# Layer norm in two parts, query weights behind x in one DMA queue, and edge counts from ScalarE signs, in a graph transformer layer

## Chip, cores, metric

One core of a Trainium2 chip runs the whole program. The metric is device time in microseconds. The kernel before was timed three times: 259.06, 259.42 and 260.69 us, median 259.42.

## What is computed

625 nodes with 256 features each, and 20,000 edges (src, dst), sorted by dst. The reference, cut to what matters:

```python
edge_index = jnp.stack([src, dst])
xn = _layernorm(x, axis=-1)                      # (x - mean) / sqrt(var + 1e-5)
x = x + gnn(xn, edge_index, W_l, W_r, b_r) + mix(xn[None], Wqkv, bqkv, Wproj, bproj, temperature)[0]
x = x + ffn(_layernorm(x, axis=-1)[None], W1, b1, Wg, bg, Wd, bd)[0]

# gnn: mean over incoming edges
sums = segment_sum(x[src], dst); counts = segment_sum(ones, dst)
out = (sums / maximum(counts, 1)) @ W_l.T + x @ W_r.T + b_r
# mix: qkv = x @ Wqkv.T + bqkv, 8 heads of 32; q and k normalised per head;
#   a Taylor-like attention: sums over nodes of (1 + s + s*s/2) * v, over the same without v; then Wproj
# ffn: H = gelu(x @ W1 + b1); gate = softmax(H @ Wg + bg); each row takes its best of 8 experts
```

## The kernel before

The nodes stand in T = 5 tiles of 125 rows. The program is written by hand for each engine: each engine has one list of instructions, and semaphores tie them. SyncE and ScalarE issue the loads.

**Front (0 to about 15 us).** SyncE loads the edges, ScalarE loads x; when x is there, SyncE issues w_qkv (L376), b_qk, w_lr and the rest. VectorE turns src and dst into floats (L653, L654), makes half_src, which ScalarE's steps need (L655), and then the first layer norm for all five tiles at once: BN_STATS (L659), BN_AGGR (L662), variance plus epsilon (L664), ScalarE's square root (L523), reciprocal (L670) and the normalised rows `xn` (L672, tile `row` in the profile). Between them VectorE makes `ge` (L666, a part of `at_sb`): for k = 1 to 4, whether each dst is at least 125 k. TensorE transposes xn (L915, two tiles of nodes at a time), ScalarE copies each part to xnT (L528), and TensorE multiplies by w_qkv (L922).

**Projections.** For t = 0 to 4 the q and k columns (`projected(t, ...)`, two 512-wide float32 products, four matmuls in the profile), then for t = 0 to 4 the v columns with W_l's. They go round four PSUM banks; so the last of the v projections needs the bank that ScalarE's first copy to vz (L535) empties. VectorE adds the bias to q and k (L694, `biased`), ScalarE squares them (L516, `square`), VectorE sums the squares by head (L699, `head_sums`), ScalarE takes the roots of the norms (L538, L539) and VectorE makes them factors and scales q and k (L723 to L733).

**Which tiles a group of edges touches.** Behind the first projection TensorE multiplies a column of ones by `ge` (L937, five matmuls summed), which gives for each of 32 groups of 625 edges how many have dst at or past each tile's start. VectorE reads the sums (L712, L713), GpSimd turns them into codes (L445 to L465), and TensorE branches on these.

**One-hot products (33 to 99.8 us).** The segment sum is a product of one-hot matrices. For each group g of 5 x 125 edges, VectorE writes five one-hot matrices of dst and two step matrices of src (L681, L684), and ScalarE three step matrices by a Sign (L501: +1 or -1 as a column is past src or not), in a ring of seven buffers in `mem`. Both call this `fill(g)`; ScalarE's fill of a group may start when TensorE has used the group seven earlier (semaphore oh_free). TensorE works in 16 pairs of groups (L958, L960, ending in L986). Between the pairs stand jobs of the attention, all through PSUM bank 7: `sums` (L992), which VectorE reads at L741 and L742, then five transposes of q and k (L999, ScalarE's copy L546), four products L1016 (VectorE's L751), and four L1021 (ScalarE's L554). Each job waits till the reader before has emptied the bank. After the last pair (L1024) the sums are complete.

ScalarE's list from the end of the front on is this:

```python
act.wait_ge(half_ready, 1)
step_rows(0, 0, 2)
act.wait_ge(var_ready, 1)
nc.scalar.activation(rstd[:, :], rstd[:, :], ACT.Sqrt).then_inc(std_ready, 1)
step_rows(0, 2, act_steps(0)).then_inc(steps_ready, 1)
...
for t in range(T):
    fill(1 + t)
    square(t)
for t in range(T):
    act.wait_ge(qkv_ps, T + t + 1)
    nc.scalar.copy(vz[:, t, 0:2 * C], ps[0:TP, QKV_BANKS[(T + t) % 4], :]).then_inc(vz_ready, 1)
...
for g in range(T + 1, AHEAD):
    fill(g)
```

The attention, the second layer norm and the experts follow and aren't touched.

## Time and profile before

| | us |
|---|---|
| median of three runs | 259.42 |
| the profiled execution | 260.61 |
| its span, first to last instruction | 258.6 |
| TensorE busy | 238.5 |
| VectorE busy | 146.5 |
| ScalarE busy | 143.1 |
| GpSimd busy | 33.1 |

Spans of instructions overlap where an engine works in a pipeline, so the step from one start to the next is often shorter than the duration of one. TensorE is busy nearly always, but that is an average; what counts is, in each stretch, who was waited for last. The timelines show it: each line has the start, the duration, the instruction, and in brackets how long the engine had stood idle and which instruction it had waited for. A line of the timeline can hold several like instructions (x5). The granted clock is TensorE's, as a share of 2.4 GHz; 0.5 is the lower level of 1.2 GHz.

### The profile page before, as it was taken

Reading aid. Unit: us, or ns where it says so; the run is one execution under the profiler, and the core shown is the slowest. Engines: PE = TensorE matmul, PEld = TensorE weight load, DVE = VectorE, ACT = ScalarE, POOL = GpSimd, SP = SyncE. Lnnn points to the kernel's source line nnn. Section 1 sums busy time; section 2 is a strip of 40 time slices with the busy share of each in tenths; the row PEclk is TensorE's granted clock in tenths of the full one; section 3 lists DMA queues with packets and bytes.
Section 4 is the critical chain, followed back from the end, with each engine's and each line's share of the span. In section 5 each row is a group of like instructions: output and inputs, shape, how many; then the busy total and the mean of one; then the engine's idle time right before and its main releaser. Section 6 shows DMA issues by size and latency. Waiting matters only on the chain.

```text
span 258.6 us, 4709 instructions
## 1 busy us (share of the span) xinstructions
PE 238.5 (92%) x1428; PEld 147.7 (57%) x1429; DVE 146.5 (57%) x418; ACT 143.1 (55%) x213; POOL 33.1 (13%) x63
## 2 busy tenths in 40 slices
PE   7599989989998989999999999998899999999990
PEld 3336647555554544433358885544355568888880
DVE  2968799999999955991114566700810242332220
ACT  3679666999999984899971014424015333332000
POOL 7007400000000005600000000000270000000331
PEclk9889999999999999999999999999999999999998
DMA  4760000000000000069950000030034000000111
GB/s 129 276 216 0 3 1 5 3 3 4 5 3 3 3 5 0 3 237 423 426 218 4 0 0 0 6 128 27 0 92 118 0 1 3 0 1 3 32 31 39
DMA packets 6030, 15.82 MB, mean 61 GB/s; under 512 B 2724, under 2 KB 3783, under 8 KB 4723
## 3 DMA queue, kind: packets, MB, share of 16 engines
q1 hardware_dynamic: 4576, 13.43, 13.9%
q0 software_dynamic: 1280, 1.31, 1.9%
q10 hardware_dynamic: 144, 0.66, 0.6%
q8 instruction: 21, 0.34, 0.6%
q14 instruction: 9, 0.07, 0.1%
HBM read 14.08 MB, written 1.30 MB: 59 GB/s over the span
## 4 chain that ended last, share of the span: by engine, by line
PE 62%; ACT 25%; DVE 8%; DMA 2%; issue 1%; POOL 0%; DVEq 0%
ACT mem L501 21%; PE ps L1223 16%; PE ps L1155 11%; PE ps L1043 7%; PE ps L1064 5%; PE ps L1121 4%; PE ps L1206 3%; PE ps L958 3%; PE ps L1112 2%; PE ps L1114 2%; DMA edges_sb<-in_edges 2%; PE ps L922 1%; PE ps L1131 1%; DVE qk_sb L733 1%; DVE mem L681 1%
## 5 line engine op out<-in xcount | busy, mean ns | idle before, releaser
L501 ACT ACTIVATE mem<-ids_m,half_src 125x628 bf16<-125x628 f16 x96 | 69.8, 817 | 5.1 <-DVE half_src L655 3.0
L958 PE MATMUL ps<-mem 125*128 125x501 bf16 x180 | 50.8, 374 | 4.3 <-issue 2.9
L681 DVE TENSOR_SCALAR mem<-node_ids,dst_f 125x628 bf16<-125x628 f16 x160 | 51.7, 369 | 0.0
L1223 PE MATMUL ps<-mem 128*125 x192 | 41.6, 379 | 0.0
L960 PE MATMUL ps<-mem 125*128 125x126 bf16 x180 | 39.3, 218 | 0.0
L1223 PEld LDWEIGHTS ps<-mem 128*125 128x125 f32 x192 | 36.0, 188 | 5.4
L958 PEld LDWEIGHTS ps<-mem 125*128 x180 | 17.6, 98 | 26.8 <-issue 10.2
L570 ACT ACTIVATE qk_sb<-ps,sc_col 125x626 f32<-125x626 f32 (+1 forms) x40 | 28.6, 779 | 3.7 <-PE ps L1043 3.7
L1155 PE MATMUL ps<-xnT,w_sb 128*128 128x512 f32 (+1 forms) x104 | 28.8, 435 | 0.1
L684 DVE TENSOR_SCALAR mem<-ids_m,src_f 125x628 bf16<-125x628 f16 x64 | 23.6, 369 | 0.0
L1155 PEld LDWEIGHTS ps<-xnT,w_sb 128*128 128x128 f32 x104 | 15.9, 191 | 13.2 <-issue 12.9
L615 ACT ACTIVATE mem<-ps,b_sb 128x625 f32<-128x625 f32 x14 | 11.0, 783 | 20.4 <-PE ps L1155 20.1
L1043 PE MATMUL ps<-mem 32*125 32x313 f32 (+1 forms) x160 | 19.1, 472 | 0.2 <-DVE mem L760 0.2
L636 ACT COPY mem<-mem 128x1000 f32 x8 | 8.2, 1031 | 19.8 <-PE ps L1223 19.8
L960 PEld LDWEIGHTS ps<-mem 125*128 x180 | 17.5, 97 | 1.5
L893 DVE SCALAR_TENSOR_TENSOR row<-vz,row x12 | 5.8, 486 | 20.1 <-issue 20.1
L484 POOL DMA_INDIRECT rows_sorted<-row,pos x5 | 6.2, 1238 | 78.9 <-DVE pos L851 77.7
L922 PE MATMUL ps<-wqkv_sb,xnT 128*125 128x512 f32 (+1 forms) x40 | 15.8, 536 | 0.0
L878 DVE COPY mem<-mem 128x500 f32 (+2 forms) x12 | 4.1, 393 | 20.3 <-ACT mem L615 19.9
L1064 PE MATMUL ps<-qk_sb,vz 125*32 125x313 f32 (+1 forms) x160 | 14.7, 439 | 0.6 <-ACT qk_sb L570 0.6
L1043 PEld LDWEIGHTS ps<-mem 32*125 32x125 f32 x160 | 8.9, 180 | 10.5 <-issue 5.0
L489 POOL DMA_INDIRECT out<-row,node_u x5 | 5.9, 1189 | 55.5 <-DVE row L896 55.5
(200 smaller groups left out, 265.0 us busy)
## 6 DMA issues: line engine op xcount, KB each, us to landing
mem<-in_wd SPq DMA_DIRECT2D x8, 1024.0 KB, 12.9
w_sb<-in_w SPq DMA_DIRECT2D x1, 1024.0 KB, 8.7
vz<-in_bd SPq DMA_DIRECT2D x1, 1000.0 KB
wqkv_sb<-in_w_qkv SPq DMA_DIRECT2D x1, 768.0 KB, 4.2
x_all<-in_x ACTq DMA_DIRECT2D x1, 640.0 KB, 4.5
row<-rows_sorted SPq DMA_DIRECT2D x1, 579.7 KB
wlr_sb<-in_w_lr SPq DMA_DIRECT2D x1, 512.0 KB, 6.0
bqk_all<-in_b_qk SPq DMA_DIRECT2D x1, 256.0 KB, 5.2
```

The costliest lines, as they stand in the source:

```text
L501: ins = nc.scalar.activation(oh[:, g % OHB, 0, j, :], ids_m1[:, :], ACT.Sign, bias=half_src[:, g * GC + j:g * GC + j + 1])
L570: nc.scalar.activation(gsq[:, u % NGB, :, 0:w], ps[0:TP, b:b + 2, 0:w], ACT.Square, bias=sc2_col[0:TP, :]).then_inc(g_ready, 1)
L615: ins = nc.scalar.activation(hT[:, k, :], psf[:, at:at + N], ACT.Gelu, bias=b1_sb[:, k:k + 1])
L681: ins = nc.vector.tensor_scalar(oh[:, g % OHB, 1, j, :], node_ids[:, :], dst_f[:, col:col + 1], None, ALU.is_equal)
L684: ins = nc.vector.tensor_scalar(oh[:, g % OHB, 0, j, :], ids_m1[:, :], src_f[:, col:col + 1], 2.0, ALU.is_ge, ALU.mult)
L922: ins = mm(ps[0:TP, QKV_BANKS[n % 4], lo:hi], xnT[:, c, TP * t:TP * (t + 1)], w[:, c, :], start=(c == 0), stop=(c == KC - 1))
L958: mm(psf[:, bass.ds(tile * BANK, TW + 1)], node_of, oh[:, buf, 0, j, 0:TW + 1], start=False, stop=False, skip_group_check=True)
L960: mm(psf[:, bass.ds(tile * P + 5 * BANK, AW)], node_of, oh[:, buf, 0, j, TW:N + 1], start=False, stop=False, skip_group_check=True)
L1043: ins = mm(ps[0:TP, 2 * ((2 * u2 + h // 2) % SLOTS) + h % 2, 0:hi - lo], kT[rows, hg, TP * m:TP * (m + 1)], qT[rows, hg, lo:hi], start=Tru ...
L1064: ins = mm(ps[D * h:D * (h + 1), 6 + k % 2, 0:hi - lo], v[:, m, P * hg + D * h:P * hg + D * (h + 1)], gsq[:, (2 * u2 + pr) % NGB, i, 0:hi ...
L1155: ins = mm(psf[:, at + lo:at + hi], w1_sb[:, c, P * k:P * (k + 1)], x2nT[:, c, lo:hi], start=(c == 0), stop=(c == KC - 1))
L1223: ins = mm(ps[0:TP, 4 + n % EB, 0:C], hT_step[:, n % EB, k, :], wd_sb[:, bass.ds(e, 1), k, :], start=(k == 0), stop=(k == KH - 1))
```

## The change

Six edits, all in the first 45 us of the program:

1. The load of w_qkv is issued by ScalarE, right behind x, and no longer by SyncE when x has landed.
2. `ge` is made by ScalarE: for each k a Sign of 2 dst + `below`, a column that GpSimd makes by one more iota. The values are then +1 and -1, so the bounds at which VectorE reads the sums change with them.
3. The matmuls over `ge` stand ahead of all transposes, behind 15 of the 18 filler products of zeros that TensorE starts with; three fillers follow. VectorE reads their sums within the layer norm.
4. The layer norm goes in two parts: tiles 0 and 1, then 2 to 4.
5. TensorE transposes the second and third part of xn behind the first and second projection.
6. ScalarE's list has the copies and roots between the steps, its fill(6) ahead of the copies to vz, and VectorE's fill(2) stands one place later.

```diff
@@ -95,6 +95,7 @@
...
+        below = sb("below", [TP, T - 1])
         erank = sb("erank", [TP, E])
...
@@ -216,6 +217,7 @@
...
+        dst_ready = sem("dst_ready")
         flag_sum = sem("flag_sum")
...
@@ -366,6 +368,7 @@
...
+        LN_PARTS = ((0, 2), (2, T))
...
@@ -373,7 +376,6 @@
...
-            sp.dma_start(wqkv_sb[:, :, :], w_qkv).then_inc(in_wqkv, 16)
             sp.dma_start(bqk_all[:, :], b_qk.partition_broadcast(P)).then_inc(in_bqk, 16)
...
@@ -413,6 +415,8 @@
...
+            nc.gpsimd.iota(below[:, :], pattern=[[-2 * TP, T - 1]], base=1 - 2 * TP, channel_multiplier=0,
+                           allow_small_or_imprecise_dtypes=True)
             nc.gpsimd.iota(thr[:, :], pattern=[[TP, T + 1]], base=0, channel_multiplier=0,
...
@@ -493,6 +497,7 @@
...
+            act.dma_start(wqkv_sb[:, :, :], w_qkv).then_inc(in_wqkv, 16)
             act.wait_ge(root_ready, 1)
...
@@ -517,19 +522,37 @@
...
-            act.wait_ge(half_ready, 1)
-            step_rows(0, 0, 2)
-            act.wait_ge(var_ready, 1)
-            nc.scalar.activation(rstd[:, :], rstd[:, :], ACT.Sqrt).then_inc(std_ready, 1)
-            step_rows(0, 2, act_steps(0)).then_inc(steps_ready, 1)
-            for j in range(3):
+            act.wait_ge(dst_ready, 1)
+            for k in range(1, T):
+                ins = nc.scalar.activation(ge[:, k - 1].rearrange("p g j -> p (g j)"), dst_f[:, :], ACT.Sign,
+                                           bias=below[:, k - 1:k], scale=2.0)
+            ins.then_inc(flag_rows, 1)
+
+            def xT_copy(j):
                 own = slice(2 * TP * j, min(2 * TP * (j + 1), N))
...
-            for t in range(T):
+
+            def root_part(n):
+                act.wait_ge(var_ready, n + 1)
+                lo, hi = LN_PARTS[n]
+                nc.scalar.activation(rstd[:, lo:hi], rstd[:, lo:hi], ACT.Sqrt).then_inc(std_ready, 1)
+
+            root_part(0)
+            act.wait_ge(half_ready, 1)
+            step_rows(0, 0, 2)
+            xT_copy(0)
+            root_part(1)
+            step_rows(0, 2, act_steps(0)).then_inc(steps_ready, 1)
+            fill(1)
+            xT_copy(1)
+            square(0)
+            xT_copy(2)
+            for t in range(1, T):
                 fill(1 + t)
...
+            fill(T + 1)
             for t in range(T):
...
@@ -537,7 +560,7 @@
...
-            for g in range(T + 1, AHEAD):
+            for g in range(T + 2, AHEAD):
                 fill(g)
...
@@ -651,26 +674,38 @@
...
-            step(nc.vector.tensor_copy(dst_f[:, :], dst_i[:, :]))
+            nc.vector.tensor_copy(dst_f[:, :], dst_i[:, :]).then_inc(dst_ready, 1)
+            dve.wait_ge(dst_ready, 1)
             nc.vector.tensor_scalar(half_src[:, :], src_f[:, :], -1.0, 0.5, ALU.mult, ALU.add).then_inc(half_ready, 1)
...
+            def variances(lo, hi):
+                for t in range(lo, hi):
+                    ins = nc.vector.bn_aggr(mv[:, t, :], bn[:, t, :])
+                step(ins)
+                nc.vector.tensor_scalar(rstd[:, lo:hi], mv[:, lo:hi, 1], LN_EPS, None, ALU.add).then_inc(var_ready, 1)
+
+            def normalised(n):
+                lo, hi = LN_PARTS[n]
+                dve.wait_ge(std_ready, n + 1)
+                step(nc.vector.reciprocal(rstd[:, lo:hi], rstd[:, lo:hi]))
+                for t in range(lo, hi):
+                    nc.vector.tensor_scalar(xn[:, t, :], x_sb[:, t, :], mv[:, t, 0:1], rstd[:, t:t + 1],
+                                            ALU.subtract, ALU.mult).then_inc(xn_ready, 1)
+
             dve.wait_ge(in_x, 16)
-            for t in range(T):
-                ins = nc.vector.bn_stats(bn[:, t, :], x_sb[:, t, :])
-            step(ins)
-            for t in range(T):
-                ins = nc.vector.bn_aggr(mv[:, t, :], bn[:, t, :])
-            step(ins)
-            nc.vector.tensor_scalar(rstd[:, :], mv[:, :, 1], LN_EPS, None, ALU.add).then_inc(var_ready, 1)
-            for k in range(1, T):
-                ins = nc.vector.tensor_scalar(ge[:, k - 1].rearrange("p g j -> p (g j)"), dst_f[:, :], float(TP * k), None,
-                                              ALU.is_ge)
-            ins.then_inc(flag_rows, 1)
-            dve.wait_ge(std_ready, 1)
-            step(nc.vector.reciprocal(rstd[:, :], rstd[:, :]))
-            for t in range(T):
-                nc.vector.tensor_scalar(xn[:, t, :], x_sb[:, t, :], mv[:, t, 0:1], rstd[:, t:t + 1],
-                                        ALU.subtract, ALU.mult).then_inc(xn_ready, 1)
+            nc.vector.bn_stats(bn[:, 0, :], x_sb[:, 0, :])
+            step(nc.vector.bn_stats(bn[:, 1, :], x_sb[:, 1, :]))
+            variances(0, 2)
+            nc.vector.bn_stats(bn[:, 2, :], x_sb[:, 2, :])
+            normalised(0)
+            nc.vector.bn_stats(bn[:, 3, :], x_sb[:, 3, :])
+            step(nc.vector.bn_stats(bn[:, 4, :], x_sb[:, 4, :]))
+            variances(2, T)
+            dve.wait_ge(flag_sum, 1)
+            past_first = ps[0:1, 0, 0:(T - 1) * NG].rearrange("p (k g) -> p k g", k=T - 1)
+            nc.vector.tensor_scalar(edge_tiles[:, 0], past_first, GC * TP - 1.0, None, ALU.is_gt)
+            nc.vector.tensor_scalar(edge_tiles[:, 1], past_first, 1.0 - GC * TP, None, ALU.is_gt).then_inc(flag_read, 1)
+            normalised(1)
             dve.wait_ge(ids_ready, 1)
...
@@ -707,19 +742,14 @@
...
-            dve.wait_ge(flag_sum, 1)
-            past_first = ps[0:1, 0, 0:(T - 1) * NG].rearrange("p (k g) -> p k g", k=T - 1)
-            nc.vector.tensor_scalar(edge_tiles[:, 0], past_first, GC * TP - 0.5, None, ALU.is_gt)
-            nc.vector.tensor_scalar(edge_tiles[:, 1], past_first, 0.5, None, ALU.is_gt).then_inc(flag_read, 1)
-
-            fill(2)
             head_sums(1)
...
+            fill(2)
             biased(4)
...
-            dve.wait_ge(std_ready, 2)
+            dve.wait_ge(std_ready, 3)
             step(nc.vector.tensor_scalar(nrm[:, :, :, :], nrm[:, :, :, :], NORM_EPS, None, ALU.max))
...
@@ -903,10 +933,17 @@
...
-            for n in range(18):
+            for n in range(15):
+                zeroed(1 + n % 3)
+            pe.wait_ge(flag_rows, 1)
+            for j in range(GC):
+                ins = mm(ps[0:1, 0, 0:(T - 1) * NG], ones_col[:, :], ge[:, :, :, j], start=(j == 0), stop=(j == GC - 1))
+            ins.then_inc(flag_sum, 1)
+            for n in range(3):
                 zeroed(1 + n % 3)
...
-            for j in range(3):
+
+            def x_transposed(j):
                 first, last = 2 * j, min(2 * j + 2, T)
...
@@ -916,6 +953,8 @@
...
+            x_transposed(0)
+
             def projected(n, t, parts):
...
@@ -931,11 +970,8 @@
...
-                if t == 0:
-                    pe.wait_ge(flag_rows, 1)
-                    for j in range(GC):
-                        ins = mm(ps[0:1, 0, 0:(T - 1) * NG], ones_col[:, :], ge[:, :, :, j], start=(j == 0), stop=(j == GC - 1))
-                    ins.then_inc(flag_sum, 1)
+                if t < 2:
+                    x_transposed(t + 1)
             pe.wait_ge(in_wlr, 16)
...
```

Three places, as the engines' lists have them; the line numbers of the changed kernel are its own. First ScalarE from its first one-hot steps (L501, L506 in the changed kernel) to the first square. Before:

```order
L501 ACTIVATE mem<-ids_m,half_src 125x628 [waits half_ready,ids_ready]
L501 ACTIVATE mem<-ids_m,half_src 125x628
L523 ACTIVATE rstd<-rstd 125x5 [waits var_ready]
L501 ACTIVATE mem<-ids_m,half_src 125x628
L528 COPY xnT<-ps 128x2x250 [waits xT_ps] x2
L528 COPY xnT<-ps 128x2x125 [waits xT_ps]
L501 ACTIVATE mem<-ids_m,half_src 125x628 x3
L516 ACTIVATE at_sb<-qk_sb 125x512 [waits qk_ready]
L501 ACTIVATE mem<-ids_m,half_src 125x628 x3
L516 ACTIVATE at_sb<-qk_sb 125x512 [waits qk_ready]
```

With the change:

```order
L527 ACTIVATE at_sb<-dst_f,below 125x160 [waits dst_ready,ids_ready]
L527 ACTIVATE at_sb<-dst_f,below 125x160 x3
L540 ACTIVATE rstd<-rstd 125x2 [waits var_ready]
L506 ACTIVATE mem<-ids_m,half_src 125x628 [waits half_ready]
L506 ACTIVATE mem<-ids_m,half_src 125x628
L534 COPY xnT<-ps 128x2x250 [waits xT_ps]
L540 ACTIVATE rstd<-rstd 125x3 [waits var_ready]
L506 ACTIVATE mem<-ids_m,half_src 125x628 x4
L534 COPY xnT<-ps 128x2x250 [waits xT_ps]
L521 ACTIVATE at_sb<-qk_sb 125x512 [waits qk_ready]
L534 COPY xnT<-ps 128x2x125 [waits xT_ps]
```

Four Signs (L527) come first, one root has become two, the first copy of transposed x stands between them, and the third copy stands behind the first square.

Next ScalarE from the last squares (`at_sb<-qk_sb`) to the copies to vz, with the roots of the norms (`nrm`). Before:

```order
L516 ACTIVATE at_sb<-qk_sb 125x512 [waits qk_ready]
L501 ACTIVATE mem<-ids_m,half_src 125x628 x3
L516 ACTIVATE at_sb<-qk_sb 125x512 [waits qk_ready]
L535 COPY vz<-ps 125x512 [waits qkv_ps]
L538 ACTIVATE nrm<-nrm 125x5x8 [waits sums_ready]
L539 ACTIVATE nrm<-nrm 125x5x8
L535 COPY vz<-ps 125x512 [waits qkv_ps] x4
L501 ACTIVATE mem<-ids_m,half_src 125x628 x3
```

With the change:

```order
L506 ACTIVATE mem<-ids_m,half_src 125x628 x3
L521 ACTIVATE at_sb<-qk_sb 125x512 [waits qk_ready]
L506 ACTIVATE mem<-ids_m,half_src 125x628 x3
L558 COPY vz<-ps 125x512 [waits qkv_ps]
L561 ACTIVATE nrm<-nrm 125x5x8 [waits sums_ready]
L562 ACTIVATE nrm<-nrm 125x5x8
L558 COPY vz<-ps 125x512 [waits qkv_ps] x4
L506 ACTIVATE mem<-ids_m,half_src 125x628 [waits oh_free]
```

One more fill, three ACTIVATEs, stands between the last square and the first copy; behind the copies one fill without a wait is gone.

Last TensorE from the fillers (`ps<-zeros`) over the transposes (`ps<-ident,row`) to the first projections (`ps<-wqkv_sb,xnT`). Before:

```order
L903 MATMUL ps<-zeros 128x512 x17
L915 MATMUL ps<-ident,row 128x125 [waits xn_ready,ident_ready]
L915 MATMUL ps<-ident,row 128x125 x3
L915 MATMUL ps<-ident,row 128x125 [waits xn_ready]
L915 MATMUL ps<-ident,row 128x125 x3
L915 MATMUL ps<-ident,row 128x125 [waits xn_ready]
L915 MATMUL ps<-ident,row 128x125
L922 MATMUL ps<-wqkv_sb,xnT 125x512 [waits xT_copied,in_wqkv]
L922 MATMUL ps<-wqkv_sb,xnT 125x512
L937 MATMUL ps<-at_sb,ones_col 1x128 [waits flag_rows]
L937 MATMUL ps<-at_sb,ones_col 1x128 x4
```

With the change:

```order
L933 MATMUL ps<-zeros 128x512 x14
L940 MATMUL ps<-at_sb,ones_col 1x128 [waits flag_rows]
L940 MATMUL ps<-at_sb,ones_col 1x128 x4
L933 MATMUL ps<-zeros 128x512 x3
L952 MATMUL ps<-ident,row 128x125 [waits xn_ready,ident_ready]
L952 MATMUL ps<-ident,row 128x125 x3
L961 MATMUL ps<-wqkv_sb,xnT 125x512 [waits xT_copied,in_wqkv]
L961 MATMUL ps<-wqkv_sb,xnT 125x512
L952 MATMUL ps<-ident,row 128x125 [waits xn_ready]
L952 MATMUL ps<-ident,row 128x125 x3
L961 MATMUL ps<-wqkv_sb,xnT 125x512 [waits xT_copied]
L961 MATMUL ps<-wqkv_sb,xnT 125x512
```

The count matmuls (`ps<-at_sb,ones_col`) are ahead of everything that needs x, and each later transpose stands behind a projection.

## Rows read from the trace of the kernel before

**Rows 1.** The page: the span, and the chain that ended last by line.

```profile
span 258.6 us, 4709 instructions
...
ACT mem L501 21%; PE ps L1223 16%; PE ps L1155 11%; PE ps L1043 7%; PE ps L1064 5%; PE ps L1121 4%; PE ps L1206 3%; PE ps L958 3%; PE ps L1112 2%; PE ps L1114 2%; DMA edges_sb<-in_edges 2%; PE ps L922 1%; PE ps L1131 1%; DVE qk_sb L733 1%; DVE mem L681 1%
```

**Rows 2.** Timeline, VectorE, 0-50, 77-83 us: start, duration, instruction, [idle before <-releaser].

```profile
5.53 1.72 DVE L659 BATCH_NORM_STATS2 bn<-x_all 125x6 f32<-125x256 f32 x5
7.29 0.45 DVE L662 BATCH_NORM_AGGREGATE mv<-bn 125x2 f32<-125x6 f32 x5
...
8.67 1.71 DVE L672 TENSOR_SCALAR row<-x_all,mv,rstd 125x256 f32<-125x256 f32 x5
...
14.70 0.69 DVE L694 TENSOR_TENSOR qk_sb<-ps,bqk_all 125x512 f32<-125x512 f32 x1 [2.27 <-PE ps L922]
...
27.83 0.38 DVE L723 TENSOR_SCALAR nrm<-nrm 125x80 f32<-125x80 f32 x1 [0.43 <-ACT nrm L539]
...
32.40 1.26 DVE L681 TENSOR_SCALAR mem<-node_ids,dst_f 125x628 bf16<-125x628 f16 x4
...
34.45 1.25 DVE L681 TENSOR_SCALAR mem<-node_ids,dst_f 125x628 bf16<-125x628 f16 x4
...
43.12 0.15 DVE L742 TENSOR_SCALAR ks<-ps 128x1 f32<-128x1 f32 x1
...
81.42 0.52 DVE L751 SCALAR_TENSOR_TENSOR yT_sb<-ps,ks,mem 128x312 f32<-128x312 f32 x1
```

**Rows 3.** Timeline, TensorE, 0-50 and 78-100 us.

```profile
9.56 1.41 PE L915 MATMUL ps<-ident,row 125*128 125x125 f32 x10 [2.75 <-DVE row L672]
10.94 3.65 PE L922 MATMUL ps<-wqkv_sb,xnT 128*125 128x512 f32 x4
...
29.19 1.03 PE L922 MATMUL ps<-wqkv_sb,xnT 128*125 128x256 f32 x4
...
33.08 0.37 PE L958 MATMUL ps<-mem 125*128 125x501 bf16 x1 [0.50 <-issue]
...
44.39 0.62 PE L999 MATMUL ps<-ident,qk_sb 125*128 125x125 f32 x4
...
82.00 0.80 PE L1021 MATMUL ps<-yT_sb,blk 128*128 128x313 f32 x2 [0.37 <-DVE yT_sb L751]
...
94.81 0.17 PE L986 MATMUL ps<-zeros 125*128 125x2 bf16 x1
```

**Rows 4.** Windows: busy us by engine, PEclk (granted clock), DMA share, GB/s.

```profile
3.40:4.40 1.00, 1.00 (x4) 0.39 (x3) 0.00 (x0) 0.00 (x0) 0.76 (x6) 1.00 1.06 430
11.00:12.00 1.00, 1.00 (x2) 0.48 (x3) 1.00 (x4) 1.00 (x3) 0.00 (x0) 0.51 0.85 310
```

**Rows 5.** Timeline, ScalarE, 0-50 us.

```profile
10.21 1.43 ACT L528 COPY xnT<-ps 128x500 f32<-128x500 f32 x3 [1.33 <-PE ps L915]
...
15.42 0.63 ACT L516 ACTIVATE at_sb<-qk_sb 125x512 f32<-125x512 f32 x1 [1.66 <-DVE qk_sb L694]
...
26.59 0.56 ACT L535 COPY vz<-ps 125x512 f32<-125x512 f32 x1
27.43 0.24 ACT L538 ACTIVATE nrm<-nrm 125x40 f32<-125x40 f32 x1 [0.28 <-DVE nrm L699]
...
45.05 0.58 ACT L546 COPY mem<-ps 128x500 f32<-128x500 f32 x1 [2.57 <-PE ps L999]
```

**Rows 6.** The chain of waits, 0-90 and 93-100 us: start, us, what.

```profile
16.05 2.13 ACT mem L501 x3
...
95.15 0.42 ACT mem L554
...
95.61 0.79 PE ps L1021 x2
```

**Rows 7.** DMA issues (KB, us to landing); timeline, GpSimd, 0-50 us.

```profile
wqkv_sb<-in_w_qkv SPq DMA_DIRECT2D x1, 768.0 KB, 4.2
...
20.29 2.21 POOL L445 TENSOR_TENSOR edge_tiles<-edge_tiles 1x128 f32<-1x128 f32 x1 [13.39 <-DVE edge_tiles L713]
```

## The prediction, made before the changed kernel was run

> **What bounds the kernel now.** I first read the page: the span is 258.6 us, and the largest line in the chain that ended last is ScalarE's L501, the one-hot steps, with 21% [rows 1]. So a part of the program is paced by ScalarE, and the change works just in front of it. Then I read the three timelines of the first 45 us side by side. Four stages are to be seen in them.
>
> (a) Front. VectorE takes the statistics of x from 5.53 and writes the normalised rows from 8.67 [rows 2]. TensorE transposes from 9.56 and projects from 10.94, and the first four projection matmuls take 3.65 us [rows 3]; the granted clock there is 0.51 [rows 4], the 1.2 GHz level, after TensorE had stood idle for 2.75 us ahead of the transposes [rows 3]. The first squaring on ScalarE can start at 15.42 [rows 5].
>
> (b) Norms. ScalarE alternates fills and squares up to 26.59, takes the roots at 27.43 [rows 5], and VectorE goes on at 27.83 [rows 2].
>
> (c) From 27.83 VectorE has no idle entry until its last fill; that is why whatever waits for VectorE later is tied to this moment. TensorE starts the one-hot products at 33.08 and reaches the first transposes of q and k at 44.39 [rows 3]; ScalarE waits 2.57 us for them and starts its unbroken stretch at 45.05 [rows 5].
>
> (d) End of the stretch. The chain shows ScalarE's third L554 ending at 95.56 and TensorE's L1021 starting at 95.61 [rows 6]. TensorE was done with the pair before it at 94.81 + 0.02 [rows 3]: without ScalarE it would have gone on 0.78 us sooner, not more. And that TensorE stretch itself began at 82.00, released by VectorE's L751, which starts at 81.42 [rows 2, 3]. So behind ScalarE stands VectorE, 0.78 us away. This decides the forecast: whatever the front saves, only 0.78 us less the shift of VectorE's 27.83 can reach the end. Behind the products nothing is changed.
>
> **The change part by part.** The rows come from one execution with a span of 258.6 us and a time of 260.61 us; 2.0 us lie around the span. The median of the runs is 259.42, 1.19 lower. I work out a difference inside the span and take it off the median.
>
> *Statistics in two parts (VectorE, ScalarE).* Five BN_STATS take 1.72 us with overlap, so 0.33 each; five BN_AGGR 0.45, so 0.09 each [rows 2]. First part: VectorE starts on x at 5.53 with 0.1 for the instruction before it, 5.6, two statistics to 6.28, two aggregates and the addition 0.37, so 6.67. The root takes about 0.2 on ScalarE beside the third BN_STATS, to 7.0; reciprocal 0.2, two rows of x at 0.33 each with a drain, 7.91. TensorE's transposes start 0.13 later, at 8.04 instead of 9.56: 1.52 earlier. ScalarE copies the first transposed part 0.65 after that as now (9.56 to 10.21 [rows 3, 5]), at 8.69, and the first projection starts at most 1.38 after the transposes (9.56 to 10.94), at 9.42.
>
> *Second part.* Two statistics, three aggregates, addition: 7.83 to 9.05. The two readings of the edge counts, which stood later, come in here, 0.2 each: 9.41. The second root follows ScalarE's copy and is ready then too. Reciprocal 0.2, three rows 0.97: 10.59. Fill(0) is 2.05 (32.40 to 34.45 [rows 2]): 12.64. The biased q and k and the start of the squaring are 0.72 (14.70 to 15.42 [rows 2, 5]): 13.36 in place of 15.42, 2.06 earlier. The four comparisons of dst, which stood on VectorE ahead of the reciprocal, are not in this sum any more, since ScalarE makes them.
>
> *Transposes 2 and 3 between the projections (TensorE).* Each now stands behind a projection. At full clock four 512-wide matmuls are half of 3.65, so 1.8; first projection 9.42 to 11.2, four transposes 0.6, and so on. VectorE wants its second tile only at 15.4, so this hides.
>
> *Four Sign instructions of 160 columns (ScalarE).* Not in the trace. Bounds: a root of 40 columns (0.14 from one start to the next) and a step of 628 columns (2.13 for three, 0.71 each [rows 6]); 0.56 to 2.84 us for four. Between them by width, 0.14 + 0.57 x 120/588: 0.26 each, 1.04 in all, 5.38 to 6.45. The first root is wanted at 6.67: hidden. At the upper end it would be 1.5 late (5.38 + 2.84 = 8.2 in place of 6.67) and with it the whole front, and the end 0.8 later than now, 260.2; I take 0.26, since 160 columns lie near the lower row. The five count matmuls and three fillers then fit before 8.04.
> The Trainium skill ("ScalarE: Activation LUTs", What ACT_TABLE_LOAD costs) gives a bias from a column a fixed 280 ns and 0.833 ns a column, with some 93 ns of overlap: an estimate of 0.32 each. By that the fillers would end some 0.15 later and the gain would be 0.15 less. The 628-column steps of the trace agree with it (0.71 by the same formula).
>
> *Fill(6) ahead of the vz copies, third copy behind the first square (ScalarE).* The order rows show both. Between the first square and the first vz copy lie 11.17 us now (15.42 to 26.59 [rows 5]). Added: one more fill, 2.13 [rows 6], and the 250-wide copy, a fifth of the 1.43 of three copies [rows 5], 0.29. The first vz copy starts at 13.36 + 11.17 + 2.13 + 0.29 = 26.95 instead of 26.59. The roots now wait for sums until 27.43; in the new order those are there long before, so the roots start behind the copy (0.56): 27.51. VectorE goes on 0.40 later (27.43 to 27.83): 27.91. **So of 2.06 us won, 2.42 are spent ahead of the roots, 0.28 of slack there pays for part, and VectorE's long stretch starts 0.08 later.** The fill isn't lost: it leaves ScalarE's time after the copies, where ScalarE waits anyway.
>
> *Last v projection (TensorE).* It reuses the bank of the first vz copy: 27.6 instead of 29.19. TensorE waits up to 1.9 us for it. From its start to the first product are 3.89 (29.19 to 33.08 [rows 3]): 31.5, 1.6 earlier. TensorE would then be at the first qk transposes at 42.8. But bank 7 is freed by VectorE's last L742 at 43.12 + 0.15 [rows 2], now 43.35. The transposes start at 43.4, 1.0 before 44.39; ScalarE's stretch starts 1.0 earlier.
>
> *End.* ScalarE's third L554 is over at 94.6. VectorE's L751 (81.42 [rows 2]) is 0.08 later, so TensorE starts its last stretch at 82.08 and reaches the last L1021 at 94.83 + 0.08 = 94.91, instead of 95.61. **Sum: -0.70 us.** VectorE's last fill ends at 94.2 (81.42 + 0.45 + six fills of 2.05) and the last pair starts at 96.0: covered.
>
> *Weights behind x in ScalarE's queue.* They took 4.2 us from their issue to landing [rows 7]. Now they follow x, which has landed by 5.5; 768 KB at the 430 GB/s of 3.4 to 4.4 us [rows 4] are 1.8 us: they land near 7.3. At the latest, if all of 4.2 follows x, it is 9.7, 0.3 after they are wanted. ScalarE's table load starts one DMA issue later, and nothing waits for it before 5.4. b_qk moves up one place in SyncE's queue. *Pool's flags:* Pool starts on the edge counts at 20.29 [rows 7] and is done before 33.08, at most 12.8 us. Now it starts at 9.5 and the flags are wanted at 31.5: even with three fills of VectorE (6.2) in its way it is done by 28.5. Its new iota of four columns stands ahead of one that ScalarE wants at 5.4: covered.
>
> **The rivals.**
> 1. *The front's gain passes through.* If ScalarE's work ahead of the roots is 1 us shorter than I count, VectorE's stretch moves with it and the 1.6 us of TensorE's first product come out: 259.42 - 1.6 = 257.8. For it: ScalarE is the chain's largest line. Against it: it must run 2.42 us of added work there, by its own rows. Chance 0.13.
> 2. *x is late (slower).* x and the weights share one queue. If the transfers share the DMA engines evenly instead of one after the other, x lands when twice its 640 KB and the 160 KB of edges are through: 1.44 MB at 430 GB/s, 3.35 us in place of 1.9, some 1.4 later. All of VectorE's front moves, the square starts at 14.8, the roots at 28.9, and VectorE's stretch 1.5 late makes the end 1.5 - 0.78 = 0.7 later: 260.1. It turns to a loss from a square later than 13.36 + 0.70 = 14.06 on. Against it: x is issued first, and no wait of the trace shows a later transfer of a queue holding up an earlier one. Chance 0.13.
> The Trainium skill ("DMA: Bandwidth & Descriptors", Queues, rings and completion order) says that an engine consumes one ring's descriptors in order but that a later one may finish first. No run here shows which.
> 3. *The clock falls once more.* TensorE idles up to 1.9 us ahead of the last v projection. Before, 2.75 us of idling was followed by the 0.51 [rows 4], which made 3.65 us of 1.8. If it falls again for as long, TensorE is at the qk transposes at 42.8 + 1.8 = 44.6 instead of 44.39: the end is 0.2 later, 259.6. For it: the same kind of gap. Against it: it is shorter.
> The Trainium skill ("TensorE: Matmul & The Clock Gate", Part 1) has the clock gated to half after idling. The trace agrees at 11 us; by that rule this rival, without it the forecast. Chance 0.12.
> 4. *The change does little.* The first projection still waits for something else and the square starts above 14: the same loss as in 2, already priced. Chance 0.04.
>
> **How the numbers follow.** The forecast, -0.70 us and so 258.7, has 0.58; its own range is 258.1 to 259.3, from some 0.3 either way at ScalarE's order ahead of the roots and as much between two executions. The range of 257.7 to 260.2 takes in the rivals and the upper end of the Sign. A measurement of this kernel can tell about 1%, 2.6 us, from no change. No case reaches 256.8: faster by over 1% 0.05, within 1% 0.90, slower 0.05.
>
> **What would show it.** Right: transposes at 8.0 to 8.2, full clock at 11 to 14, first square at 13.3 to 13.6, fill(6) ahead of the vz copies, nrm roots near 27.5, TensorE idle ahead of the last v projection, first product near 31.5, ScalarE's stretch from 44, TensorE waiting for VectorE's L751 near 82, and the products' end 0.7 earlier than before. Wrong: roots before 26.7 (rival 1) or after 28.2 (rival 2); a granted clock of half at 28 to 32 (rival 3); a change of more than 1 us behind the products, where no edit stands.

## The result, and the profile after

The changed kernel takes 261.49 us (median of 20 runs, 260.98 to 262.56), the kernel before 259.26 us in 20 runs. The ratio is 1.0075, with a 95% interval of 1.0058 to 1.0092: slower by 0.8%, where 0.70 us less was forecast. The profiled execution took 262.11 us, with a span of 259.0; the median span of the 20 runs is 259.45.

The page of the changed kernel, its span and the chain that ended last by line:

```profile
span 259.0 us, 4713 instructions
...
ACT mem L506 20%; PE ps L1259 16%; PE ps L1191 11%; PE ps L1079 7%; PE ps L1100 5%; PE ps L994 5%; PE ps L1157 4%; PE ps L1242 3%; PE ps L933 3%; PE ps L1148 2%; PE ps L1150 2%; DVE mem L716 1%; PE ps L1167 1%; PE ps L996 1%; PE ps L1129 1%
```

It hardly differs from [rows 1], so the page can't tell what changed; the timelines can. ScalarE's, which answers to [rows 5]:

```profile
5.69 1.39 ACT L527 ACTIVATE at_sb<-dst_f,below 125x160 bf16<-125x160 f32 x4 [2.47 <-DVE dst_f L677]
7.05 0.20 ACT L540 ACTIVATE rstd<-rstd 125x2 f32<-125x2 f32 x1
...
9.25 0.58 ACT L534 COPY xnT<-ps 128x500 f32<-128x500 f32 x1 [0.58 <-PE ps L952]
9.72 0.21 ACT L540 ACTIVATE rstd<-rstd 125x3 f32<-125x3 f32 x1
...
14.03 0.63 ACT L521 ACTIVATE at_sb<-qk_sb 125x512 f32<-125x512 f32 x1 [0.81 <-DVE qk_sb L729]
...
17.59 0.63 ACT L521 ACTIVATE at_sb<-qk_sb 125x512 f32<-125x512 f32 x1 [0.54 <-DVE qk_sb L729]
...
26.07 2.22 ACT L506 ACTIVATE mem<-ids_m,half_src 125x628 bf16<-125x628 f16 x3
28.20 0.56 ACT L558 COPY vz<-ps 125x512 f32<-125x512 f32 x1
28.66 0.24 ACT L561 ACTIVATE nrm<-nrm 125x40 f32<-125x40 f32 x1
...
45.16 0.58 ACT L569 COPY mem<-ps 128x500 f32<-128x500 f32 x1 [2.34 <-PE ps L1035]
```

Four things are to be seen. The first square is at 14.03, not at 13.36. The second one waited 0.54 for VectorE, which no step of mine had. Fill(6) stands at 26.07, ahead of the copy to vz, as the order said. The norms' roots start at 28.66 without a wait; before they started at 27.43 and waited.

VectorE's timeline, for [rows 2]:

```profile
5.79 0.42 DVE L696 BATCH_NORM_STATS2 bn<-x_all 125x6 f32<-125x256 f32 x1
...
9.96 0.18 DVE L690 RECIPROCAL rstd<-rstd 125x3 f32<-125x3 f32 x1 [0.15 <-ACT rstd L540]
...
11.20 1.27 DVE L716 TENSOR_SCALAR mem<-node_ids,dst_f 125x628 bf16<-125x628 f16 x4
...
13.32 0.68 DVE L729 TENSOR_TENSOR qk_sb<-ps,bqk_all 125x512 f32<-125x512 f32 x1
13.92 1.80 DVE L716 TENSOR_SCALAR mem<-node_ids,dst_f 125x628 bf16<-125x628 f16 x4
...
15.98 0.68 DVE L716 TENSOR_SCALAR mem<-node_ids,dst_f 125x628 bf16<-125x628 f16 x1
...
16.88 0.68 DVE L729 TENSOR_TENSOR qk_sb<-ps,bqk_all 125x512 f32<-125x512 f32 x1
...
29.05 0.20 DVE L753 TENSOR_SCALAR nrm<-nrm 125x80 f32<-125x80 f32 x1 [2.17 <-ACT nrm L562]
...
44.04 0.14 DVE L772 TENSOR_SCALAR ks<-ps 128x1 f32<-128x1 f32 x1
...
82.34 0.52 DVE L781 SCALAR_TENSOR_TENSOR yT_sb<-ps,ks,mem 128x312 f32<-128x312 f32 x1
```

VectorE goes on at 29.05, behind 2.17 us of waiting for the roots, where it was 27.83. Its fill(0) takes 2.12 (11.20 to 13.32), but its fill(1), the same seven instructions, 2.96 (13.92 to 16.88); the four L716 take 1.80 in place of 1.27, and the one at 15.98 takes 0.68. What ran beside it is GpSimd's work on the flags, which [rows 7] had at 20.29:

```profile
9.97 0.44 POOL L449 TENSOR_TENSOR edge_tiles<-edge_tiles 1x128 f32<-1x128 f32 x1 [3.08 <-DVE edge_tiles L707]
...
14.49 0.66 POOL L462 TENSOR_SCALAR between<-between 1x160 f32<-1x160 f32 x1
15.23 0.65 POOL L463 TENSOR_SCALAR tile_of<-tile_of 1x160 f32<-1x160 f32 x1
15.96 0.52 POOL L464 TENSOR_TENSOR tile_of<-tile_of,between 1x160 f32<-1x160 f32 x1
...
17.50 0.31 POOL L469 CAST more<-tile_of 1x160 int32<-1x160 f32 x1
```

The first of these instructions takes 0.44 here; in [rows 7], where VectorE's fill(2) was running (20.06 to 22.11), it took 2.21. So the rows of before already had the two engines in each other's way, only with GpSimd as the one that waited.

TensorE's timeline, for [rows 3], and its windows, for [rows 4] (each line: the stretch and its length, then the busy time of each engine, the granted clock and the DMA share):

```profile
7.96 0.82 PE L933 MATMUL ps<-zeros 125*128 125x512 bf16 x3
8.62 0.59 PE L952 MATMUL ps<-ident,row 125*128 125x125 f32 x4
9.97 1.95 PE L961 MATMUL ps<-wqkv_sb,xnT 128*125 128x512 f32 x4 [0.76 <-ACT xnT L534]
...
28.81 1.13 PE L961 MATMUL ps<-wqkv_sb,xnT 128*125 128x256 f32 x4 [2.47 <-ACT vz L558]
...
33.22 0.57 PE L994 MATMUL ps<-mem 125*128 125x501 bf16 x1
...
82.92 0.80 PE L1057 MATMUL ps<-yT_sb,blk 128*128 128x313 f32 x2 [0.28 <-DVE yT_sb L781]
...
96.10 0.79 PE L1057 MATMUL ps<-yT_sb,blk 128*128 128x312 f32 x2 [0.16 <-ACT mem L577]
```

```profile
11.00:12.00 1.00, 1.00 (x6) 0.47 (x5) 1.00 (x4) 1.00 (x3) 0.83 (x3) 1.00 0.33 97
...
31.00:32.00 1.00, 0.75 (x3) 0.11 (x2) 1.00 (x2) 0.59 (x1) 0.00 (x0) 0.50 0.00 0
32.00:33.00 1.00, 1.00 (x3) 0.18 (x2) 1.00 (x3) 0.00 (x0) 0.00 (x0) 0.50 0.00 0
```

The first projection runs at full clock (four matmuls in 1.95 instead of 3.65). Later TensorE idles 2.47 us ahead of the last v projection, and the granted clock is 0.50, the 1.2 GHz level, at 31 to 33. At the end of the stretch ScalarE is only 0.16 late (0.63 before), and TensorE's last L1057 is at 96.10, against 95.61 before and 94.91 forecast.

### The profile page after: what moved, and what is told of

Same layout as the page of the kernel before. It is cut to its first block, busy times and chain, and to the rows that moved or that the text cites. A ratio compares the mean times of both kernels' runs of the same rounds, so it can differ in the third digit from the quotient of the medians.

```text
span 259.0 us, 4713 instructions
## 1 busy us (share of the span) xinstructions
PE 239.4 (92%) x1428; PEld 147.7 (57%) x1429; DVE 147.3 (57%) x416; ACT 144.2 (56%) x218; POOL 31.9 (12%) x64
## 4 chain that ended last, share of the span: by engine, by line
PE 67%; ACT 24%; DVE 5%; issue 2%; POOL 1%; DVEq 0%; POOLq 0%
ACT mem L506 20%; PE ps L1259 16%; PE ps L1191 11%; PE ps L1079 7%; PE ps L1100 5%; PE ps L994 5%; PE ps L1157 4%; PE ps L1242 3%; PE ps L933 3%; PE ps L1148 2%; PE ps L1150 2%; DVE mem L716 1%; PE ps L1167 1%; PE ps L996 1%; PE ps L1129 1%
## 5 line engine op out<-in xcount | busy, mean ns | idle before, releaser
L506 ACT ACTIVATE mem<-ids_m,half_src 125x628 bf16<-125x628 f16 x96 | 69.7, 812 | 4.5 <-PE ps L1022 4.5
L716 DVE TENSOR_SCALAR mem<-node_ids,dst_f 125x628 bf16<-125x628 f16 x160 | 52.5, 372 | 0.0
L1191 PEld LDWEIGHTS ps<-xnT,w_sb 128*128 128x128 f32 x104 | 15.9, 191 | 13.2 <-issue 12.9
L961 PE MATMUL ps<-wqkv_sb,xnT 128*125 128x512 f32 (+1 forms) x40 | 14.2, 490 | 3.2 <-ACT vz L558 2.5
```

The costliest lines, as they stand in the source:

```text
L506: ins = nc.scalar.activation(oh[:, g % OHB, 0, j, :], ids_m1[:, :], ACT.Sign, bias=half_src[:, g * GC + j:g * GC + j + 1])
L716: ins = nc.vector.tensor_scalar(oh[:, g % OHB, 1, j, :], node_ids[:, :], dst_f[:, col:col + 1], None, ALU.is_equal)
L961: ins = mm(ps[0:TP, QKV_BANKS[n % 4], lo:hi], xnT[:, c, TP * t:TP * (t + 1)], w[:, c, :], start=(c == 0), stop=(c == KC - 1))
L1191: ins = mm(psf[:, at + lo:at + hi], w1_sb[:, c, P * k:P * (k + 1)], x2nT[:, c, lo:hi], start=(c == 0), stop=(c == KC - 1))
```

## The experiments

In what follows "roots" is the start of ScalarE's first `nrm` root and "go-on" the start of VectorE's first instruction behind it. Eleven experiments ran, in three groups on three chips: 1 to 4, 5 to 8, 9 to 11. Each group has its own 29 runs of the kernel before (medians 259.20, 260.19 and 260.01). These medians differ because the runs of the kernel before fall into two groups of spans (see 4 and 5), so spans are compared beside the ratios.

**1. Fill(6) behind the copies again.** The changed kernel with

```diff
-            fill(T + 1)
             for t in range(T):
                 act.wait_ge(qkv_ps, T + t + 1)
...
-            for g in range(T + 2, AHEAD):
+            for g in range(T + 1, AHEAD):
```

> The changed kernel with fill(6) of ScalarE put back behind the copies to vz. Theory A (the roots of the norms were pushed back by ScalarE work ahead of them, and VectorE's long stretch hangs on the roots): the first vz copy starts 2.1 us sooner (26.1 instead of 28.2), the roots wait for the head sums and start near 26.9, VectorE goes on near 27.3 instead of 29.05, and the time falls by 1.5 to 1.8 us to about 259.8. Theory B (ScalarE's place in the order is hidden; the loss comes from TensorE's clock or from the start): within 0.5 us of 261.5.

Measured: 259.47 us, ratio to the kernel before 1.0013 [0.9992, 1.0034]; spans 257.2 to 257.7, against 259.0 to 259.9 of the changed kernel. ScalarE's timeline in it:

```profile
26.08 0.56 ACT L557 COPY vz<-ps 125x512 f32<-125x512 f32 x1
26.93 0.24 ACT L560 ACTIVATE nrm<-nrm 125x40 f32<-125x40 f32 x1 [0.28 <-DVE nrm L733]
```

The roots are 1.73 earlier and the time 2.0 lower. One edit carries most of the loss.

**2. GpSimd's flags later.** The changed kernel with one more wait, so that GpSimd starts behind VectorE's fill(1):

```diff
             pool.wait_ge(flag_read, 1)
+            pool.wait_ge(qk_ready, 2)
```

> The changed kernel with GpSimd's work on the edge counts held back until two tiles of q and k are biased. Theory A (GpSimd beside VectorE's fill(1) slows that fill from 2.05 to 2.96 us, and ScalarE's second square waits 0.54 us for it): fill(1) takes 2.1 us again, the wait goes, all behind it is 0.5 earlier, time 0.3 to 0.5 us less. Theory B (the fill is slow for another reason, such as the DMAs of that time): fill(1) stays at 2.9 and the time is the same.

Measured: 260.60 us, ratio 1.0050 [1.0030, 1.0071]; median span 258.55, 0.9 below the changed kernel. VectorE and then ScalarE in it:

```profile
13.60 1.25 DVE L717 TENSOR_SCALAR mem<-node_ids,dst_f 125x628 bf16<-125x628 f16 x4
...
18.62 1.60 DVE L717 TENSOR_SCALAR mem<-node_ids,dst_f 125x628 bf16<-125x628 f16 x4
20.15 0.67 DVE L720 TENSOR_SCALAR mem<-ids_m,src_f 125x628 bf16<-125x628 f16 x1
```

```profile
16.64 0.62 ACT L522 ACTIVATE at_sb<-qk_sb 125x512 f32<-125x512 f32 x1
...
27.69 0.24 ACT L562 ACTIVATE nrm<-nrm 125x40 f32<-125x40 f32 x1
```

Fill(1) is back at 2.04 (13.60 to 15.64), the second square doesn't wait, and now fill(2), which has GpSimd beside it, is the slow one; there it costs nothing, since VectorE waits later in the stage anyway. The slowing follows GpSimd's instructions. The gain is more than the 0.3 to 0.5 that I expected. Part of the 0.9 may be the group of runs: experiment 3, on the same chip as 2, has a median span of 259.25, 0.7 above. The cleanest pair is 1 and 6, which differ by this wait alone and whose statistics start at 5.81 and 5.78: the roots are 0.81 apart, 0.17 of it ahead of the first square (fill(0) had been slowed too, by 0.07) and the rest behind it.
The Trainium skill ("SBUF — State Buffer", Who interferes with whom) says that VectorE in a two-port mode and GpSimd can't use their shared ports at once, and that the later of the two blocks until the other has finished. The trace agrees in kind: VectorE's 0.38 us instruction took 0.68 beside GpSimd's 0.52 us L464, and in [rows 7] it was GpSimd that waited. No trace tells which mode VectorE was in.

**3. The half clock ahead of the products filled.** The changed kernel with ten products of zeros ahead of the last v projection's wait:

```diff
                 else:
+                    for n in range(10):
+                        zeroed(1 + n % 3)
                     pe.wait_ge(vz_ready, 1)
```

> The changed kernel with ten filler products of zeros in the gap of 2.5 us ahead of the last v projection. Theory A (VectorE's stretch sets the end): the granted clock stays 1.0 from 29 to 34 us, the first one-hot product starts 1.5 us earlier (31.7 instead of 33.2), and the time falls by at most 0.3 us, because TensorE then waits for VectorE at bank 7 and at L1057. Theory C (the clock that falls at 30 us is what costs): the time falls by 1.2 to 1.7 us.

Measured: 261.41 us in 6 runs, ratio 1.0090 [1.0054, 1.0125], median span 259.25: no change from the changed kernel that 6 runs could tell. The windows of it:

```profile
30.00:32.00 2.00, 1.54 (x8) 0.86 (x7) 1.93 (x6) 1.38 (x3) 0.00 (x0) 1.00 0.00 0
32.00:34.00 2.00, 1.50 (x10) 0.65 (x9) 2.00 (x5) 0.00 (x0) 0.00 (x0) 1.00 0.00 0
```

The clock stayed full, as theory A says, and next to nothing was won. Its loads landed 0.35 later than in the changed kernel's profile, so its times are read from the start of the v projection or from the go-on. TensorE's first one-hot product starts 3.98 behind the v projection (29.15 to 33.13) in place of 4.41, and ScalarE's stretch 15.86 behind the go-on in place of 16.11. So the half clock costs some 0.4 us there, and not the 1.5 that I had expected. It doesn't reach the end: the span is the go-on plus 230.1 here and plus 230.0 with the half clock (see the table further down). The fall is real and hidden behind VectorE.

**4 and 5. What the kernel before does without its half clock.** The runs of the kernel before have two groups of spans. In the first 29 runs, 24 lie at 256.8 to 257.6 with a mean clock of 0.991 to 0.998, and 5 at 258.7 to 259.0 with 0.988 to 0.990; in later groups 13 and 12 of 29 lie high. The profiled execution behind [rows 1] to [rows 7] was a high one (258.6, 0.990). Experiment 4 is the kernel before with more products of zeros:

```diff
-            for n in range(18):
+            for n in range(30):
```

> The kernel before with 30 fillers instead of 18, so that TensorE has work up to about 9.2 us. The 20 runs of the kernel before stand in two heaps, near 259.0 and near 260.7. Theory D (the heaps differ by whether the clock falls to half after the idle time of 6.8 to 9.5, which the profiled run of 260.6 shows): every run is in the lower heap, 258.6 to 259.4, the clock is 1.0 from 10 to 15 us, and the first square starts near 13.7. Theory E (the heaps are of another cause): the runs scatter as before and the median is within 0.3 us of before's.

Measured: 259.52 us, ratio 1.0007 [0.9986, 1.0028]; spans 256.9 to 257.8 in all 12 runs, none high. That is in theory D's favour, though 0 of 12 against 5 of 29 is weak by itself. Two of its numbers missed: the first square is at 14.48, not near 13.7, and the median is above the lower heap's 259.4. The fillers last until 10.50 and themselves delay the transposes to 10.34, so nothing is won over a low run.

Experiment 5 is the kernel before, unchanged, for a second profile.

> The kernel before once more, for its trace. Its 29 timed runs have spans of 256.8 to 257.6 us at a granted clock of 0.991 to 0.998 (24 of them), or of 258.7 to 259.0 at 0.988 to 0.990 (5). Theory D (the shown trace is one of the few in which the clock fell at 11 us): a span near 257.1, the clock 1.0 from 10 to 15 us, the first four projection matmuls in 1.9 us instead of 3.65, the first square near 13.7 instead of 15.42, and the roots of the norms near 25.8 instead of 27.43. Theory E (the clock falls every time, and the heaps come from the tail of the program): half clock at 11 to 14 again also with a span near 257.

Measured: 258.63 us, span 256.8, clock 0.995. TensorE, a window and ScalarE in it:

```profile
1.38 5.92 PE L903 MATMUL ps<-zeros 125*128 125x512 bf16 x18 [1.38 <-POOL zeros L410]
9.48 1.41 PE L915 MATMUL ps<-ident,row 125*128 125x125 f32 x10 [2.19 <-DVE row L672]
10.86 1.95 PE L922 MATMUL ps<-wqkv_sb,xnT 128*125 128x512 f32 x4
```

```profile
11.00:12.00 1.00, 1.00 (x3) 0.50 (x4) 1.00 (x5) 1.00 (x3) 0.00 (x0) 1.00 0.88 249
```

```profile
13.65 0.63 ACT L516 ACTIVATE at_sb<-qk_sb 125x512 f32<-125x512 f32 x1
...
25.66 0.23 ACT L538 ACTIVATE nrm<-nrm 125x40 f32<-125x40 f32 x1 [0.28 <-DVE nrm L699]
...
43.29 0.58 ACT L546 COPY mem<-ps 128x500 f32<-128x500 f32 x1 [2.57 <-PE ps L999]
```

Against [rows 3 to 5]: the same program, the first square 1.77 earlier, the roots 1.77 earlier, ScalarE's stretch 1.76 earlier, the span 1.8 shorter. The half clock of [rows 4] is worth about that much (3.65 less 1.95 are 1.70, and the statistics start 0.08 earlier), and most executions don't have it: 57 of the 87 runs of the kernel before lie in the low group.

What TensorE did ahead of the transposes differs too. In the profile behind [rows 3] the 18 fillers are

```profile
1.38 5.43 PE L903 MATMUL ps<-zeros 125*128 125x512 bf16 x18 [1.38 <-POOL zeros L410]
```

The same 18 products end at 6.81 there and at 7.30 here. In both they first follow each other 0.43 us apart and later 0.21 us apart, and the later that begins, the longer they last and the shorter is the idling ahead of the transposes. The four profiles with this front are in one order: fillers of 5.43 us and 2.75 of idling, and 5.61 and 2.73 (experiment 9), with the half clock behind them; 5.92 and 2.19, and 6.64 and 1.73 (experiment 8), without.

**6. Both losses undone together** (the edits of 1 and 2).

> The changed kernel with both: fill(6) back behind the copies to vz, and GpSimd's work on the counts held until two tiles of q and k are biased. Theory A (the two losses add on the way to the roots): the roots near 26.0 instead of 28.66, span 256.5, time near 258.6, 0.5 us less than before. Theory B (without fill(6) another wait binds and the Pool's part is hidden): as with fill(6) alone, 259.5.

Measured: 258.63 us, ratio 0.9957 [0.9928, 0.9986]; median span 256.6. The interval lies below 1, and none of the 12 spans (256.3 to 257.6) lies in the high group. ScalarE in it:

```profile
26.12 0.24 ACT L561 ACTIVATE nrm<-nrm 125x40 f32<-125x40 f32 x1 [0.28 <-DVE nrm L734]
...
42.37 0.58 ACT L569 COPY mem<-ps 128x500 f32<-128x500 f32 x1 [2.93 <-PE ps L1035]
```

The two losses add: median spans 259.45, less 2.05 (fill), less 0.90 (flags), make 256.5.
How much faster it is depends on the runs that it is compared with. The median 260.19 lies between the two groups (13 of the 29 are high). Against the median span of the 16 low runs, 257.1, it is 0.5 us, or 0.2%; the rest of the 0.4% is that it has no high runs. And what is won against a low run isn't the front: the roots are 0.46 later than in 5 (26.12 against 25.66), but ScalarE's stretch starts 0.92 earlier (42.37 against 43.29).

**7. The counts as before.** The version of 1 (fill(6) back) with `ge` made by VectorE's four comparisons behind the first bias addition, the count matmuls behind the third projection, and the bounds as before. Its core:

```diff
             biased(0)
+            for k in range(1, T):
+                ins = nc.vector.tensor_scalar(ge[:, k - 1].rearrange("p g j -> p (g j)"), dst_f[:, :], float(TP * k), None,
+                                              ALU.is_ge)
+            ins.then_inc(flag_rows, 1)
             fill(1)
```

> The changed kernel with fill(6) back and with the edge counts as before: compared by VectorE (behind the first biased tile), counted by TensorE behind the third projection, read behind the fourth biased tile. What stays of the change: layer norm in two parts, transposes between projections, weights behind x. Theory A (the four Signs, 1.39 us on ScalarE, hold the first root back by 0.3 us, the reading of the counts holds VectorE by 0.4, and GpSimd slows fill(1)): the first square 0.6 to 0.8 us earlier than 14.03, all of it reaches the roots, span 256.3 to 256.6, time 258.4. Theory B (the front is set by x's landing and TensorE's fillers): the first square stays near 13.9 and the time is that of fill(6) alone, 259.5.

Measured: 258.89 us, ratio 0.9967 [0.9944, 0.9990]; median span 257.0. The first square is at 13.79, 0.26 earlier than in 1, and not the 0.6 to 0.8 that I expected: the Signs and the counts hardly delay the front. The first root is at 7.14 without them and at 7.05 with them. Fill(1) takes its normal 2.04. Putting the counts back and delaying the flags are two cures of one loss; the second is 0.4 better.

**8. The weights behind x alone.** The kernel before with

```diff
-            sp.dma_start(wqkv_sb[:, :, :], w_qkv).then_inc(in_wqkv, 16)
...
             act.dma_start(x_all[:, :, :], x).then_inc(in_x, 16)
+            act.dma_start(wqkv_sb[:, :, :], w_qkv).then_inc(in_wqkv, 16)
```

> The kernel before with only the load of the query weights moved behind x in ScalarE's queue. Theory A (the weights were never waited for, and x isn't delayed by them): time within 0.3 us of before's 259.2, the statistics start at 5.5 to 5.8. Theory F (the weights, now running beside the edges and x, make these land later): the float casts of the edges and the statistics of x start 0.2 us or more later in the profile and the time rises by as much.

Measured: 260.52 us, ratio 1.0017 [0.9990, 1.0044]; five spans at 256.8 to 257.4, seven at 258.3 to 259.1, the same two groups. The low runs of the two kernels agree (median spans 257.0 and 257.1): the edit costs nothing that these runs show, as theory A says. The statistics of x start at 5.72, 0.27 later than in 5.

**9. Fill(6) ahead of the copies, alone, in the kernel before** (experiment 1 reversed, on the other kernel).

> The kernel before with one edit: ScalarE's fill(6) ahead of the copies to vz. Theory A (the 2.13 us of the fill stand ahead of the norms' roots, and VectorE's stretch that hangs on them sets the end once it begins later than some 26.8 us): roots at 27.6 to 27.8 instead of 25.66, VectorE at 28.0 to 28.2; the changed kernel had 29.05 there and a span of 259.4, so here the span is 258.3 to 258.6 and the time 1.2 to 1.5 us above the kernel before. Theory B (the fill costs its whole length in any kernel): 2.1 us above. Theory C, as in my prediction (it only leaves time in which ScalarE waits anyway): within 0.3 us.

Measured: 260.36 us, ratio 1.0030 [0.9999, 1.0061], which mixes the two groups of spans of both kernels (12 of the 29 runs of before are high here). Nine of its runs have spans of 257.9 to 258.6, median 258.5, where the kernel before has 257.2 in its 17 low runs: +1.3, as theory A says, not 2.1 and not 0. The profiled one is of the three high ones:

```profile
15.40 0.63 ACT L516 ACTIVATE at_sb<-qk_sb 125x512 f32<-125x512 f32 x1 [1.47 <-DVE qk_sb L695]
...
26.57 2.23 ACT L501 ACTIVATE mem<-ids_m,half_src 125x628 bf16<-125x628 f16 x3
...
29.16 0.23 ACT L539 ACTIVATE nrm<-nrm 125x40 f32<-125x40 f32 x1
```

Its first square is where [rows 5] has it, and its roots are 1.73 later.

**10 and 11. Can the front give more?** Ten is the version of 6 with w_qkv issued by SyncE again (the edit of 8 reversed). Eleven is that with one filler in place of three behind the counts:

```diff
-            for n in range(3):
+            for n in range(1):
                 zeroed(1 + n % 3)
```

> The version with fill(6) back and GpSimd's flags late, and w_qkv issued again by SyncE when x has landed. Theory A (the weights behind x made edges and x land 0.2 us later): VectorE's casts and the statistics 0.2 us earlier, first square at 13.6 to 13.7 instead of 13.88, roots at 25.9, time 0 to 0.2 us below the version with the weights behind x, whose span was 256.6. Rival (weights landing later hold the first projection): TensorE's first projection later than 10.3, square at 14 or later, time 0.3 us or more above.

> As the version just before, with one filler product in place of three between the counts and the first transposes. Theory A (the fillers, not VectorE's rows, hold the first transposes): transposes 0.3 to 0.4 us earlier, at 8.1 to 8.3, and the first square 0.1 to 0.4 us earlier; time 0 to 0.3 us lower. Rival (the second part of the layer norm and ScalarE's list set the first square): transposes earlier, square and time unchanged.

Measured: 258.78 us, ratio 0.9950 [0.9925, 0.9976], and 258.70 us, ratio 0.9947 [0.9923, 0.9971]; median spans 256.7 and 256.6, as in 6. Neither edit moves the time. In ten the statistics start at 5.56, in eleven, with the same loads, at 5.79: two executions of one arrangement differ nearly as much as 8 and 5 do, so a delay of x by the weights isn't shown. That also makes ten a poor partner for eleven, although both start the transposes at 8.37 and 8.38. Experiment 6 has x as early as eleven (statistics at 5.78); its weights land earlier, but the transposes don't need them. There the three fillers hold the transposes until 8.59: one filler makes them 0.21 earlier and the first square 0.17 earlier (13.88 to 13.71). So theory A of eleven is right in the profile, on a small scale, and what it wins is too little for the median. In eleven the first projection (9.76) is released by the landing of the weights, so with the late issue an earlier front would wait for the weights.

## Why the prediction was wrong

The measured time is 2.79 us above the forecast. It comes in three pieces, from the prediction's own steps.

**"I work out a difference inside the span and take it off the median": 1.19 us.** The difference was counted against an execution with the half clock in its front [rows 4], which most executions don't have (experiment 5). My 2.06 us for the first square contained 1.77 us that the median had already. The sign was on the page before the run: the profiled execution lay 1.19 above the median, the prediction says so, and 0.51 stands in the rows as a term of the sum. Had I added the 2.0 us around the span to my 257.9, I would have said 259.9. Against the low executions the first square became 0.38 later (13.65 to 14.03), not earlier. What the two-part layer norm wins there, 0.9 us at the transposes (9.48 to 8.62), goes into fill(0), which now follows the later second part: in experiment 5 VectorE waits 0.58 for TensorE ahead of its first bias addition, in the changed kernel it comes to it from fill(0) without a wait.

**The products' end, "94.91": 96.10 measured, 1.19 us.** Its steps:
- First square 13.36, measured 14.03: +0.67. The statistics start 0.19 later; the first root is at 7.05 instead of 6.67; the transposes and ScalarE's copy are 0.6 late. A part of that is "The five count matmuls and three fillers then fit before 8.04": they end at 8.62, where VectorE's two rows were written by 8.22; experiment 11 against 6 puts 0.2 on it. "The second root follows ScalarE's copy and is ready then too" was right that it follows, but VectorE didn't find it ready: it waited 0.15 and went on at 9.96 instead of 9.41. Fill(0) took 2.12.
- "even with three fills of VectorE (6.2) in its way it is done by 28.5." That asks only whether GpSimd is in time, and it was (17.8). It doesn't ask what GpSimd does to VectorE, and that is what cost: fill(1) 0.9 longer, the second square 0.54 late, none of it in the sum. Experiments 2 and 6 put 0.7 to 0.9 us on it.
- "2.42 are spent ahead of the roots": right. From the first square to the vz copy are 14.17, of which 13.6 were counted and 0.54 are that wait. Roots 28.66 = 27.51 + 0.67 + 0.54 less 0.06.
- Behind the roots: VectorE's go-on 29.05 (27.91 forecast), its last reading 82.34 (81.5); its stretch was 0.30 shorter than the 53.59 of before. From TensorE's start behind that reading (82.92) to its last L1057 are 13.18, where 12.83 were counted: ScalarE was still 0.16 late.

**The rest, some 0.4 us,** is the profiled execution against the others: 259.0 is the lowest span of the 20, whose median is 259.45.

Right was the reading of what stands behind ScalarE, "VectorE, 0.78 us away". The profiled executions bear it out; the last column is the span less VectorE's go-on:

| kernel | go-on | last L1021 or L1057 | span | difference |
|---|---|---|---|---|
| before, profiled | 27.83 | 95.61 | 258.6 | 230.8 |
| 4 | 26.88 | 94.58 | 257.5 | 230.6 |
| 5, before again | 26.05 | 93.83 | 256.8 | 230.8 |
| 8 | 26.32 | 94.09 | 257.0 | 230.7 |
| changed | 29.05 | 96.10 | 259.0 | 230.0 |
| 1 | 27.32 | 94.34 | 257.3 | 230.0 |
| 2 | 28.08 | 95.19 | 258.2 | 230.1 |
| 3 | 29.39 | 96.50 | 259.5 | 230.1 |
| 6 | 26.51 | 93.54 | 256.5 | 230.0 |
| 7 | 26.75 | 94.03 | 257.0 | 230.3 |
| 9 | 29.56 | 96.67 | 259.6 | 230.0 |
| 10 | 26.32 | 93.50 | 256.5 | 230.2 |
| 11 | 26.36 | 93.42 | 256.4 | 230.0 |

Where fill(6) or the early layer norm has made VectorE the last, the end is its go-on plus 230.0 to 230.3. In the kernel before, and in 4 and 8, it is up to 0.75 more, because there ScalarE's stretch is the later one (it starts 17.2 behind the go-on, in the others 15.9 to 16.7): that is the slack, and it is why experiment 9 costs 1.3 and not 2.1 us. "The fill isn't lost" was therefore wrong once the front's gain was not there: the edit was to be paid from 2.06 us that the median run didn't have.

Of the rivals, number 3 came true as a mechanism (0.50 after 2.47 us of idling) and not in its price (experiment 3: 0.4 at the first product, nothing at the end). Number 2 named the right point of decision, a square later than 14.06, but counted from the high execution; with the square at 14.03 the change lost already. Its mechanism, a late x, was at most 0.2 to 0.3 us and isn't shown apart from scatter. Number 1 didn't happen. What I lacked was a rival on the state of the profiled execution itself. The Signs were little trouble: four in 1.39 us against 1.04 counted. They end at 7.08, as VectorE's addition ahead of the root does (7.02), so they hide; only the counts behind them come later than I had them.
The Trainium skill ("ScalarE: Activation LUTs", What ACT_TABLE_LOAD costs) made them an estimate of 0.32 each; from the first Sign to the root are 1.36, so 0.34: nearer than my 0.26.

What stays open: why the same fillers become fast earlier in one execution than in another (in four profiles that went with the longer idling and with the half clock, and no experiment separates the two); and the exact split of the first square's 0.38 us between loads, counts and the second part of the layer norm.
